# Split operands for cross attention's values and for batch 1's first feed-forward product, and another order in pair 3

## The reference

```python
# block 0: cross attention (16 heads of 8), then a feed-forward layer
out = attention(x, ctx) @ Wo + bo
h = (out - mean) * rsqrt(var + eps) * ln_g + ln_b
h = gelu(h @ W1 + b1, approximate=False)        # 128 -> 512
x = x + out + h @ W2 + b2
# block 1: 16 heads of 64
x = attn(ln(x, g1, b1), ln(x, g1, b1), Wq1, Wk1, Wv1, Wo1, bo1) + x
x = attn(ln(x, g2, b2), ctx, Wq2, Wk2, Wv2, Wo2, bo2) + x   # v = ctx @ Wv2: 154 rows, 96 -> 1024
x = geglu_ff(ln(x, g3, b3), Wp, bp, Wf, bf) + x
```

## Time and profile before

| | us |
|---|---|
| median of 3 runs | 460.51 |
| lowest and highest | 460.4 and 461.62 |
| the profiled execution: time | 461.69 |
| the profiled execution: span on the core | 459.9 |
| granted TensorE clock, mean over the span | 0.996 |
| TensorE busy | 440.5 (96%) |
| VectorE, ScalarE, GpSimd busy | 277.9, 239.3, 214.8 |

### The profile page before, as it was taken

The page is one execution under the profiler, slowest core; times in us unless marked ns, Lnnn a source line. Parts: engine busy times, 40 slices in busy tenths (PEclk is TensorE's granted clock), DMA queues, the critical chain, the costliest instruction groups (busy, mean ns, idle before and its releaser), DMA issues.

```text
span 459.9 us, 7026 instructions
## 1 busy us (share of the span) xinstructions
PE 440.5 (96%) x2758; PEld 261.3 (57%) x2758; DVE 277.9 (60%) x510; ACT 239.3 (52%) x324; POOL 214.8 (47%) x186
## 2 busy tenths in 40 slices
PE   7998898899999999999999999999999999999896
PEld 4644454565645656655545765545575554754696
DVE  2766636576864586457656848447735677553753
ACT  3853564455557366556445526456416665237632
POOL 4587101026883796444566636873226444255010
PEclk9998999999999999999999999999999999999999
DMA  8600000000000100000001010020001000000000
GB/s 235 226 1 2 1 1 0 0 1 1 0 1 0 36 1 0 0 1 1 1 1 46 2 34 1 2 68 1 0 9 40 0 2 1 1 1 1 0 19 29
DMA packets 7985, 8.89 MB, mean 19 GB/s; under 512 B 561, under 2 KB 6129, under 8 KB 7953
## 3 DMA queue, kind: packets, MB, share of 16 engines
q1 hardware_dynamic: 7952, 8.45, 6.0%
HBM read 7.92 MB, written 0.52 MB: 18 GB/s over the span
## 4 chain that ended last, share of the span: by engine, by line
PE 85%; DVE 7%; ACT 5%; issue 2%; DMA 1%; SPq 0%; DVEq 0%
PE PV L744 18%; PE ST L715 15%; PE ST L637 11%; PE M L688 7%; PE ST L717 5%; PE M L792 5%; PE DEN L759 3%; ACT PT L1301 2%; PE ST L653 2%; PE ST L529 2%; PE M L834 2%; DVE maxw L1499 1%; PE ST L355 1%; PE DEN L482 1%; PE ST L677 1%
## 5 line engine op out<-in xcount | busy, mean ns | idle before, releaser
L1144 POOL TENSOR_TENSOR psums<-PT 128x1024 f32<-128x1024 f32 (+1 forms) x32 | 76.1, 2379 | 132.1 <-ACT PT L1301 131.9
L1301 ACT ACTIVATE PT<-ST 128x1024 f32<-128x1024 f32 (+1 forms) x96 | 98.1, 1025 | 37.7 <-PE ST L717 36.1
L715 PE MATMUL ST<-R 64*128 64x512 f32 (+1 forms) x576 | 104.9, 405 | 0.0
L1641 DVE TENSOR_REDUCE maxw<-M 128x1 f32<-128x512 f32 x128 | 83.5, 687 | 33.1 <-PE M L688 32.8
L744 PE MATMUL PV<-PT,V 128*64 128x512 f32 (+1 forms) x384 | 89.5, 601 | 0.0
L1148 POOL TENSOR_TENSOR psums<-psums,PT 128x1024 f32<-128x1024 f32 x32 | 76.0, 2374 | 2.5
L688 PE MATMUL M<-R 64*128 64x512 f32 (+1 forms) x256 | 71.1, 361 | 0.9 <-DVE AT L1525 0.4
L715 PEld LDWEIGHTS ST<-R 64*128 64x128 f32 (+1 forms) x576 | 57.6, 171 | 14.1 <-ACT PT L1301 8.2
L688 PEld LDWEIGHTS M<-R 64*128 64x128 f32 x256 | 37.0, 184 | 36.1 <-issue 25.2
L744 PEld LDWEIGHTS PV<-PT,V 128*64 128x64 f32 (+1 forms) x384 | 24.7, 136 | 53.4 <-issue 51.1
L1309 ACT ACTIVATE AT<-PV 128x512 f32<-128x512 f32 x32 | 19.1, 598 | 62.3 <-PE PV L744 62.3
(11 more groups left out here) (246 smaller groups left out, 662.0 us busy)
## 6 DMA issues: line engine op xcount, KB each, us to landing
Wo<-in_wo SPq DMA_DIRECT2D x2, 512.0 KB, 6.3
xnT<-in_xT SPq DMA_DIRECT2D x2, 256.0 KB, 3.5
psums<-in_sel SPq DMA_DIRECT2D x1, 512.0 KB, 6.6
X<-in_x SPq DMA_DIRECT2D x1, 512.0 KB, 7.9
w<-in_w SPq DMA_DIRECT2D x2, 256.0 KB, 8.0
PT<-in_wq SPq DMA_DIRECT2D x1, 512.0 KB, 8.7
PT<-in_wk SPq DMA_DIRECT2D x1, 512.0 KB, 8.4
PT<-in_wv SPq DMA_DIRECT2D x1, 512.0 KB, 7.8
```

Of the source, the lines that this page charges most:

```text
L715: return pe.matmul(u[0:ph.KC, h, :], R[head(h), g % 3, part_k, 1, k], R[head(h), g % 3, part_q, 0, :], start=(n == 0), stop=False)
L1144: ins = pool.tensor_tensor(s, p[:, 0], p[:, 1], ALU.add)
L1301: act.activation(PT1[0:ph.KC, g % 2, c], bank(("st", g, c))[0:ph.KC, :, :], ACT.Exp, scale=HD ** -0.5).then_inc(ph.exp, 1)
L1641: ins = dve.tensor_reduce(maxw[:, g % 2, 0, at:at + 1], m[:, :], AX, ALU.max, negate=True)
```

## The change

It does five things.

1. **Values of cross attention** (`values(1, t)`, `g` = 8 to 11): the two float32 products of a step become six `fp32r` products through `three`. For it the context is split once on GpSimd at `g` = 6 (`split_operand(ctx2, ...)`, 96x308), and `Wv2` at `g` = 7, the leading part on ScalarE, the trailing one on VectorE (96x1024 each), into the tile `Wv`, which self attention's values no longer need by then.
2. **Hidden features of batch 1** (`hidden(1)`, `g` = 3): four float32 products become twelve `fp32r` ones. `W1` is split on GpSimd at `g` = 0 (128x512). The features are split at `g` = 2: ScalarE writes them twice (`xh`, then `xnT`), VectorE computes the difference `xl` (`trailing_first`) behind `trailing(4)` and ahead of the maxima of pair 4.
3. **Order in pair 3 on TensorE**: `project(5)` now stands ahead of `hidden(1)`, and the second half of `hidden(1)` behind the first piece of `weigh(3)`.
4. **Order in pair 3 on ScalarE**: `leading(5)` now stands ahead of the two table loads and the gelus.
5. **Order in pair 3 on VectorE**: `trailing(5)` now stands ahead of `maxima_rows(4)`.

The diff, its context cut short:

```diff
@@ -80,6 +80,7 @@
         work = sb("work", [P, 2, N])
+        parts = sb("parts", [P, 2, FF], F32R)
         lnv = sb("lnv", [P, TB, 1])
@@ -97,6 +98,7 @@
         Wv2 = w12[0:C, :]
+        ctx2 = parts[0:C, :, 0:B * S]
         Wk2 = w12[0:C, :]
@@ -220,8 +222,11 @@
         var_done = [sem(f"var_done{i}") for i in range(4)]
-        split_w = {k: sem(f"split_{k}") for k in ("q1", "k1", "v1", "q2", "wp")}
-        high_w = {k: sem(f"high_{k}") for k in ("q2", "wp")}
+        split_w = {k: sem(f"split_{k}") for k in ("q1", "k1", "v1", "v2", "q2", "wp")}
+        high_w = {k: sem(f"high_{k}") for k in ("v2", "q2", "wp")}
+        w1_split = sem("w1_split")
+        ctx_split = sem("ctx_split")
+        xfirst_done = sem("xfirst_done")
         full_done1 = [sem(f"xfull{i}_done") for i in range(3)]
@@ -342,6 +347,13 @@
                     pe.matmul(dst[:, 0:N // 2], zeros, work[:, 1, 0:N // 2], start=True, stop=True)
+
+            def three(dst, stationary, moving):
+
+
+                for n, (v, w) in enumerate(((0, 0), (1, 0), (0, 1))):
+                    ins = pe.matmul(dst, stationary[v], moving[w], start=(n == 0), stop=(n == 2))
+                return ins
 
@@ -518,15 +530,23 @@
 
-            def hidden(b):
-
-                loaded("w1")
-                pe.wait_ge(xn_done[0], b + 1)
-                for n in (2 * b, 2 * b + 1):
+            def hidden(b, *halves):
+
+                if b == 0:
+                    loaded("w1")
+                    pe.wait_ge(xn_done[0], 1)
+                else:
+                    pe.wait_ge(w1_split, 1)
+                    pe.wait_ge(xfirst_done, 1)
+                for n in (2 * b + k for k in halves or (0, 1)):
                     u = claim(("w1", n), gelu_done, 2 * (n + 1))
...
                         m = 2 * (n % 2) + mm
-                        ins = pe.matmul(u[:, mm, :], w1[:, m * P:(m + 1) * P], xnT[:, b * N:(b + 1) * N], start=True, stop=True)
+                        k, x = slice(m * P, (m + 1) * P), slice(b * N, (b + 1) * N)
+                        if b == 0:
+                            ins = pe.matmul(u[:, mm, :], w1[:, k], xnT[:, x], start=True, stop=True)
+                        else:
+                            ins = three(u[:, mm, :], (parts[:, 0, k], parts[:, 1, k]), (xh[:, x], xl[:, x]))
                     ins.then_inc(w1_done, 1)
@@ -630,19 +650,15 @@
 
-            def three(dst, stationary, moving):
-
-
-                for n, (v, w) in enumerate(((0, 0), (1, 0), (0, 1))):
-                    ins = pe.matmul(dst, stationary[v], moving[w], start=(n == 0), stop=(n == 2))
-                return ins
-
             def values(n, t):
...
                     pe.wait_ge(xl_done[0], t // TB + 1)
+                else:
+                    pe.wait_ge(ctx_split, 1)
+                    pe.wait_ge(split_w["v2"], 1)
                 u = claim(("v", n, t), va_done[n], t + 1)
@@ -650,7 +666,7 @@
                     else:
-                        ins = pe.matmul(u[0:r, v, :], ctxT[:, k], Wv2[:, c], start=True, stop=True)
+                        ins = three(u[0:r, v, :], (ctx2[:, 0, k], ctx2[:, 1, k]), (Wv[0:C, 0, c], Wv[0:C, 1, c]))
                 ins.then_inc(v_done[n], 1)
@@ -892,12 +908,8 @@
 
-                if g == 3:
-                    hidden(1)
                 if g in VALUES:
                     n, t = VALUES[g]
-                    if n == 1:
-                        loaded("wv2")
                     values(n, t)
@@ -935,12 +947,16 @@
                         project(g + 2)
+                    if g == 3:
+                        hidden(1, 0)
                     turn_pair(g + 1)
...
                         weigh(g, c)
+                        if g == 3 and c == 0:
+                            hidden(1, 1)
                     if g == 21:
@@ -1090,6 +1106,15 @@
 
+            def split_operand(dst, whole, done):
+
+                if done is w1_split:
+                    pool.wait_ge(ld["w1"], 16)
+                else:
+                    pool.wait_ge(w1_done, 4)
+                link(pool.tensor_copy(dst[:, 0, :], whole))
+                pool.tensor_tensor(dst[:, 1, :], whole, dst[:, 0, :].bitcast(F32), ALU.subtract).then_inc(done, 1)
+
             def add_first(b):
@@ -1131,6 +1156,8 @@
                     add_bias(1, "bo1", 1)
+                if g == 6:
+                    split_operand(ctx2, ctxT[:, 0:B * S], ctx_split)
                 if g in (13, 21):
@@ -1147,6 +1174,8 @@
                 ins.then_inc(ph.sum, 1)
+                if g == 0:
+                    split_operand(parts, w1, w1_split)
                 if g == 14:
@@ -1269,6 +1298,8 @@
                                    scale=cols[:, g:g + 1], bias=cols[:, c:c + 1]).then_inc(full_done1[n - 1], 1)
+                if n == 0 and b == 1:
+                    act.activation(xh[:, k], turned, ACT.Identity, scale=cols[:, g:g + 1], bias=cols[:, c:c + 1])
                 act.activation(xnT[:, k] if n == 0 else xh[:, k], turned, ACT.Identity,
@@ -1335,15 +1366,15 @@
                         weighted(g - 1)
-                    if g == 3:
-                        act.preload_act_table_set("gelu_and_others")
-                        gelus(1)
                     if g in VALUES:
...
                         leading(g + 2)
+                    if g == 3:
+                        act.preload_act_table_set("gelu_and_others")
+                        gelus(1)
                     if g == 0:
@@ -1356,6 +1387,8 @@
                         inverse_guess(g // 8 - 1)
+                    if g == 7:
+                        leading_weights("v2", Wv[0:C], Wv2)
                     if g == 12:
@@ -1390,8 +1423,8 @@
 
-                act.wait_ge(ld["wq2" if key == "q2" else "wp"], 16)
-                act.wait_ge(*((v_done[0], NT) if key == "q2" else (self_att.proj, NPAIR)))
+                act.wait_ge(ld["w" + key if key != "wp" else key], 16)
+                act.wait_ge(*{"v2": (v_done[0], NT), "q2": (v_done[1], TB), "wp": (self_att.proj, NPAIR)}[key])
                 act.activation(dst[:, 0, :], whole, ACT.Copy).then_inc(high_w[key], 1)
@@ -1613,6 +1646,12 @@
 
+            def trailing_first():
+
+                dve.wait_ge(xn_done[0], B)
+                dve.tensor_tensor(xl[:, N:2 * N], xnT[:, N:2 * N], xh[:, N:2 * N].bitcast(F32),
+                                  ALU.subtract).then_inc(xfirst_done, 1)
+
             def trailing_weights(key, dst, whole):
@@ -1713,9 +1752,11 @@
                         trailing_weights("wp", Wk, wp)
+                    if g == 3:
+                        trailing(5)
                     if g + 1 < NG:
                         maxima_rows(g + 1)
-                    if g + 2 < NG:
+                    if g + 2 < NG and g != 3:
                         trailing(g + 2)
@@ -1723,8 +1764,12 @@
                         second_out(1)
+                    if g == 2:
+                        trailing_first()
                     if g == 5:
                         trailing_features(1, 1)
+                    if g == 7:
+                        trailing_weights("v2", Wv[0:C], Wv2)
                     if g == 13:
```

## The result

| | before | changed |
|---|---|---|
| median of 20 runs each, us | 461.13 | 460.12 |
| lowest and highest | 459.72 and 462.22 | 457.54 and 460.95 |
| ratio of the times, 95% interval | | 0.9966 [0.9953, 0.9979] |
| the profiled execution: time | 461.69 | 460.78 |
| the profiled execution: span | 459.9 | 459.0 |

The changed kernel is faster by 0.34% (the interval goes from 0.21% to 0.47%). The forecast was 458.7 against 460.51, which is 0.40% less, and "faster by over 0.3%" was its likeliest case. The measured time lies inside the wide range (457.8 to 460.7) and outside the forecast's own (457.9 to 459.3); the ratio of 0.9966, put on the 460.51 that the forecast started from, is 458.9 and lies inside both. Of the 1.45 us between the forecast and the measured median, 0.62 come from that starting point: the kernel before had 460.51 in the three executions that I knew and 461.13 here.

The account below looks back on a forecast made before the run. TensorE was taken to bound the kernel; 1.20 us from cross attention's values plus 0.64 us from pair 3 make 1.84 us, so 460.51 - 1.84 = 458.67, say 458.7 us. Range 457.8 to 460.7 us, the forecast's own 457.9 to 459.3.

Parts of the forecast that it names:

- What bounds the kernel: Whole kernel: TensorE, busy 440.5 of 459.9 us; each microsecond it issues less is saved unless another engine is late.
- Values: Cross attention's values: six fp32r records take 1.95 us a step instead of 2.25; four steps gain 1.20 us.
- The ring of banks: Cross attention's values: if the ring held TensorE, the gain would be 0; the prediction said it doesn't.
- Hidden features and the order in pair 3: Pair 3, up to pair 4's first product: 8.27 us instead of 8.91, a gain of 0.64 us.
- I add 0.1 us for a tie: Pair 3: projection's bank freed and TensorE arriving both at 140.62; the allowance raises 8.17 to 8.27 us.
- transpose and weights by values 3.79: Pair 3: this work keeps its 3.79 us though half the hidden features, 1.50 us, is put after its first quarter.
- Rival 2: Pair 3's new order gives nothing, through slower hand-overs or start costs; only the values' 1.20 us remain: 459.3 us, chance 0.13.
- the wait at the gelus: Pair 3 before: the projection's first weight load idles 0.75 us until ScalarE's gelus end; the wait itself near 0.1 us.
- Rival 1: Pairs 2 and 5: GpSimd keeps the port between instructions, 2.8 us lost: 461.5 us, chance 0.08; first place alone 460.3, 0.09.
- the semaphore wait between the adds: Pair 2, GpSimd's two adds: argued as the reason VectorE gets the port between them, with `xl` done at 131.4.
- Rival 3: Pair 5: VectorE asks for the port before the second add, saving pair 6's 0.22 us too: 458.3 us, chance 0.08.
- Splits beside other work: Splits of `W1`, context, `Wv2` and features fit into other engines' idle time: cost 0; the features at pair 2 riskiest.

Follow-up runs that it names:

- e1_values_only: Changed kernel with the hidden-feature split and pair 3's order taken back, only the values changed: 458.84 against 459.95 us, ratio 0.9983.
- e6_no_interleave: Changed kernel with both halves of the hidden features in one piece ahead of the transpose: 459.71 us in one execution, pair 3's place 9.32 us.
- e5_order_only: Kernel before with only pair 3's new order, float32 operands kept: 461.96 us in one execution, pair 3's place 9.07 us.
- e4_split_old_order: Kernel before with hidden features from split operands, pair 3 in the old order, float32 values: 462.12 us in one execution, pair 3's place 8.91 us.
- e7_xl_twice: Changed kernel with pair 2's feature difference `xl` computed twice in a row: 461.49 us in one execution, pair 3's stretch 2.05 us longer.
- e2_hidden_only: Changed kernel with the values and their splits taken back, only hidden features and pair 3's order changed: 460.03 against 459.95 us, ratio 0.9997.
- e8_changed_again: Changed kernel without any edit, run again beside the version with filled gaps: 459.99 us, ratio 0.998 to the kernel before.

## Why the prediction was right, and where it was not

- **What bounds the kernel** was right: what TensorE issues less of is gone from the trace, in two places, and from nowhere else.
- **Values**: 1.31 us for a forecast of 1.20. The term was mis-sized by 0.03 us a step: I took the pace of the wide operand (1.95), and the step with the 96x77 one took 1.91 (`e1_values_only` has the same sum in another execution). The ring of banks held nothing up.
- **Hidden features and the order in pair 3**: 0.48 us for 0.64. This is the step that failed, in its size. The term "I add 0.1 us for a tie" named the wrong thing: there was no tie, since TensorE had 0.15 us to spare. What I left out is the cut itself. I had written "transpose and weights by values 3.79" for a product in two pieces and 1.50 us for the half between them; they are 3.96 and 1.57. `e6_no_interleave` and `e5_order_only` show both ends of this seam. Rival 2 had it among its reasons ("the halves between weights by values cost their starts") and priced it at the whole gain; it took a quarter.
- **Neither edit alone**: the split is worth nothing in the old order (8.91 us) and the order costs 0.16 us without the split. My sum had counted the wait at the gelus as "near 0.1 us", which is true of before; with the split it would have become 0.56 us (`e4_split_old_order`), and it is the order that avoids it. The sum was right since it took both together.
- **Rival 1** is refuted in both places: VectorE got in ahead of GpSimd's second add, which waits for a semaphore, and of the cast, which doesn't. What I held against it, the semaphore wait between the adds, is not what decides, as the cast shows. Its price was nearly right (`e7_xl_twice`: 2.05 us for maxima 2.3 us late, where I had 1.6 for 2.0). The Trainium skill says in "SBUF — State Buffer", section "Who interferes with whom", that whoever issues first keeps the shared pair for the whole instruction; the four instances here agree: `xl` took 2.66 to 2.75 us, and in the three where GpSimd had something to do next, this was 0.35 us (the add, twice) or 0.54 us (the cast, by my estimate) longer for it.
- **Rival 3** did not come: pair 6's scores took 5.57 us again, since VectorE asked for the port 0.3 us into the second add as before, and its first maxima there (171.59) again began some 0.5 us after their product (171.06).
- **Splits beside other work**: all at no cost in the trace, which `e1_values_only` and `e2_hidden_only` bear out pair by pair.
- **Not in the prediction**: the clock at the end. The sum of the places is 1.79 us, 0.05 from the forecast's 1.84, and 1.79 of 461.13 would be a ratio of 0.9961. With 13 executions in 32 losing 1.6 us there, 0.65 us on the average would be given back, which makes 0.9975; the measured 0.9966 and 0.998 lie on both sides of it. That the median of 460.12 us lies in the stated range is in part due to the range's width: 461.13 - 1.79 is 459.34, outside the forecast's own range by a hair, and half clock in 8 of these 20 executions, 0.64 us on the average, makes most of the rest. The prediction could have asked about the clock: it put down the 1.18 us by which the profiled execution lay above the median to the spread, and 0.9 of them were the half clock in block 0. What is shown: filling the gaps takes the half clock away in the changed kernel and changes nothing in the kernel before. What stays open: why the changed kernel meets it in 4 of 10 executions and the kernel before, with the same two gaps, almost never. Nothing there was changed but the point in time, and each part alone has it hardly or not at all (values only 1 of 12, and in its profile it lay in the same place; hidden features only 0 of 12), though these ran in rounds of their own, without the changed kernel and its unfilled gaps beside them. I have no run that tells what in the change brings it.

The fastest version is the changed kernel with the gaps filled: 458.24, 459.11 and 458.13 us, ratios of 0.996, 0.9959 and 0.9956 to the kernel before, where the changed kernel had 0.9966 and 0.998. It is clear of the kernel before each time; its lead over the changed kernel is less sure, since the intervals of the two ratios overlap, and they ran in the same rounds only once (459.11 against 459.99).

## What to carry to other kernels

A cheaper product is worth its price only if the bank that comes after it is free by then: look up which engine holds it, and move the step that frees it before you count. A product cut in two by another kind of product costs a start at each seam (0.23 us here for one insertion), so a cut must bring more than that. And when a small gain shows in the trace and not in the time, compare the granted clock in the stretches that were not touched.

## What the hardware showed that I had not expected

- VectorE, waiting for the port that it shares with GpSimd, gets it between two instructions of GpSimd even where the second follows at once and waits for nothing (171.07: the cast took 0.90 us instead of 0.36).
- TensorE's granted clock can fall to half in the middle of dense work: 18 records of the last output product in 3.4 us instead of 32, right behind waits of 1.08 and 0.42 us, in some executions and not in others of the same kernel (`e8_changed_again` has the same waits and full clock).
- Two waits that together last 1.5 us could so cost as much again, 1.6 us, in the work behind them; three products that nothing reads (six records), put into the waits, cost nothing that can be measured (kernel before: 1.0006 [0.9984, 1.0028]) and took it away.
- Ahead of all that differs between the kernels, one execution can be 2.5 us behind another (9.05 or 11.60 us to the same product): the first weights landed 0.9 us later, and TensorE's first records kept twice their later spacing until 11.2 us instead of 6.9.
